# First-layer attention: value products grouped by four heads, and the inverse of the softmax sums split between VectorE and GpSimd

## What is computed

```python
q = (x @ Wq + bq)                      # 32 heads of 16
k, v = ctx @ Wk + bk, ctx @ Wv + bv    # 8 heads of 16
scores = einsum('bkgld,bksd->bkgls', q, k) * scale + mask
attn = softmax(scores)
out = einsum('bkgls,bksd->bkgld', attn, v)
x = layer_norm(out @ Wo + bo + x) * gamma + beta
```

## Time and profile before

| | |
|---|---|
| median of 3 runs | 2901.85 us (2900.69 to 2907.3) |
| the profiled execution | 2904.45 us, its span 2902.6 us |
| granted PE clock, mean of the span | 0.963 |
| busy over the span | PE 94%, DVE 62%, ACT 52%, POOL 45% |
| first-layer loop, batch 0 | from about 53 to 331 us |
| first-layer loop, batch 1 | from about 1500 to 1775 us |

### The profile page before, as it was taken

How to read it: one execution, slowest core, us unless ns; L and a number is a source line. 1 busy time by engine, 2 the same in 40 slices (tenths; PEclk the granted TensorE clock), 3 DMA queues, 4 the chain that set the end, 5 groups by cost and what they waited for, 6 DMA issues and landing times.

```text
span 2902.6 us, 50288 instructions
## 1 busy us (share of the span) xinstructions
PE 2717.9 (94%) x17432; PEld 2168.3 (75%) x17432; DVE 1785.8 (62%) x2626; ACT 1518.5 (52%) x2360; POOL 1312.9 (45%) x710
## 2 busy tenths in 40 slices
PE   6999979999978999997979999899999789999979
PEld 5666668888866888886856666688888668888867
DVE  5999765665645665664159997566566456656541
ACT  3888534455434455543438884445554344554533
POOL 2720036566533566654428101356665335665633
PEclk8999989999998999998979999899999899999989
DMA  8410004435321344441463000135444124454512
GB/s 202 133 43 2 31 20 123 112 101 127 104 66 45 101 121 108 122 115 50 160 133 130 33 2 30 38 105 125 103 126 112 44 53 115 99 128 104 126 37 79
DMA packets 87732, 261.94 MB, mean 90 GB/s; under 512 B 19697, under 2 KB 33281, under 8 KB 81169
## 3 DMA queue, kind: packets, MB, share of 16 engines
q1 hardware_dynamic: 87568, 259.80, 34.2%
HBM read 135.45 MB, written 6.83 MB: 49 GB/s over the span
## 4 chain that ended last, share of the span: by engine, by line
issue 53%; POOL 32%; PE 9%; DMA 2%; DVE 2%; SPq 1%; POOLq 1%; ACT 0%; DVEq 0%; ACTq 0%
POOL pT L459 15%; POOL wa L459 5%; PE ps_m L902 4%; POOL v L459 4%; PE ps_s L902 3%; POOL wo L459 2%; POOL acc L511 2%; POOL wob L507 2%; DMA scr_q<-parts 1%; PE ps_m L1139 1%; POOL x_res L482 1%; DMA acc<-in_rows 1%; SPq L337 1%; DVE hT L1377 0%; POOL z L534 0%
## 5 line engine op out<-in xcount | busy, mean ns | idle before, releaser
L459 POOL TENSOR_TENSOR pT<-pT,pT 128x1024 fp32r<-128x1024 f32 x224 | 538.9, 2407 | 510.5 <-ACT pT L605 509.5
L732 ACT ACTIVATE p<-ps_s,nm 128x1024 f32<-128x1024 f32 x256 | 283.9, 1109 | 292.6 <-DVE nm L1509 292.4
L605 ACT ACTIVATE pT<-pT 128x1024 fp32r<-128x1024 f32 x224 | 237.8, 1062 | 360.1 <-DMA pT<-pb 360.1
L902 PE MATMUL ps_s<-kT,qT 128*128 128x512 f32 x1536 | 400.3, 399 | 6.5 <-ACT p L732 5.7
L459 POOL TENSOR_TENSOR wa<-stg_qk,wa 128x1024 fp32r<-128x1024 f32 x80 | 190.5, 2399 | 373.9 <-ACT wa L605 373.9
L1525 DVE STREAM_TRANSPOSE pb<-p 128x1024 f32<-128x1024 f32 x224 | 278.3, 1242 | 110.0 <-ACT p L732 100.5
L902 PEld LDWEIGHTS ps_s<-kT,qT 128*128 128x128 f32 x1536 | 281.8, 190 | 75.8 <-ACT p L732 19.6
L1506 DVE TENSOR_REDUCE nmx<-ps_s 128x1 f32<-128x1024 f32 x256 | 309.4, 1209 | 33.3 <-PE ps_s L902 33.3
L1433 DVE CUSTOM_DVE_ANT_0 sm<-ps_s,mask 128x1024 f32<-128x1024 f32 x256 | 309.2, 1209 | 20.3 <-PE ps_s L1009 12.0
L685 ACT ACTIVATE p<-sm,nm 128x1024 f32<-128x1024 f32 x256 | 293.2, 1145 | 45.1 <-DVE nm L1433 42.2
L1022 PE MATMUL ps_t<-ident,p 128*128 128x128 f32 x2048 | 288.2, 284 | 14.2 <-DVE pt L1441 7.9
(11 more groups left out here) (133 smaller groups left out, 4244.0 us busy)
## 6 DMA issues: line engine op xcount, KB each, us to landing
pT<-pb SPq DMA_DIRECT2D x896, 128.0 KB, 2.4
stg_qk<-in_wqk SPq DMA_DIRECT2D x40, 1024.0 KB, 7.6
stg_vo<-in_wo SPq DMA_DIRECT2D x48, 512.0 KB, 3.5
wob<-in_wo SPq DMA_DIRECT2D x32, 512.0 KB, 3.6
stg_vo<-in_wv SPq DMA_DIRECT2D x32, 512.0 KB, 3.6
q_stack<-scr_q SPq DMA_DIRECT2D x48, 128.0 KB, 4.4
st_ctx<-in_ctxT SPq DMA_DIRECT2D x8, 512.0 KB, 5.7
mask<-in_mask SPq DMA_DIRECT2D x2, 2048.0 KB, 12.7
```

What stands on the lines that cost most here:

```text
L459: return nc.gpsimd.tensor_tensor(out, x, f32(hi), ALU.subtract)
L605: return nc.scalar.activation(out, in_, ACT.Copy)
L732: nc.scalar.activation(p[t % 2][:], ps_s[t % 2][:], ACT.Exp, bias=nm[:, i:i + 1], scale=SCALE1, accum_out=sums[:, i:i + 1]).then_inc(exp_d ...
L902: mm = nc.tensor.matmul(out, lhs(x, c), rhs(y, c), start=start and c == 0 and i == 0, stop=stop and c == n_tiles - 1 and i == 2)
```

## The change

Three things change in the first-layer loop.

1. PE no longer makes one call values0 in each step. In every fourth step (t % 4 == 3) it makes all four calls, 64 matmuls, for the group before. The call with i = 3 stands at the same step as before.
2. DVE inverts the eight sums alone, into a new buffer rz0 (128 x 2 x 8). GpSimd writes r0 from it: it adds a broadcast zero to a broadcast rz0.
3. GpSimd's loop goes over units: value_rows(u), then the wait for rz0 of unit u, then the spread. The value rows stood ahead of everything in one run before.

ACT's wait for the buffer z0 is now on the small inverse.

```diff
+        rz0 = sb("rz0", [P, 2, UNIT], F32)
@@ GpSimd
-                for f in range(V_B):
-                    value_rows(f)
+                u0 = b * UNITS0
+                for u in range(UNITS0):
+                    value_rows(u)
+
+                    pool.wait_ge(rz0_done, u0 + u + 1)
+                    if u >= 2:
+                        pool.wait_ge(rb0_filled, u0 + u - 1)
+                    nc.gpsimd.tensor_tensor(r0[u % 2][:], rz0[:, u % 2, :].unsqueeze(2).to_broadcast([P, UNIT, HD]),
+                                            zero[:].unsqueeze(2).to_broadcast([P, UNIT, HD]), ALU.add)\
+                        .then_inc(r0_done, 1)
@@ ACT
-                        act.wait_ge(r0_done, b * UNITS0 + u - 1)
+                        act.wait_ge(rz0_done, b * UNITS0 + u - 1)
@@ PE
-                    if t >= GROUPS:
-                        values0(t // GROUPS * GROUPS - GROUPS, t % GROUPS)
+                    if t >= GROUPS and t % GROUPS == GROUPS - 1:
+                        for i in range(4):
+                            values0(t // GROUPS * GROUPS - GROUPS, i)
@@ DVE
                 def inverse(u):
                     dve.wait_ge(exp0_done, t0 + (u + 1) * UNIT)
                     if u >= 2:
-                        dve.wait_ge(rb0_filled, u0 + u - 1)
-                    nc.vector.reciprocal(r0[u % 2][:], z0[:, u % 2, :].unsqueeze(2).to_broadcast([P, UNIT, HD]))\
-                        .then_inc(r0_done, 1)
+                        dve.wait_ge(r0_done, u0 + u - 1)
+                    nc.vector.reciprocal(rz0[:, u % 2, :], z0[:, u % 2, :]).then_inc(rz0_done, 1)
```

More of the change, by code:

```diff
@@ L224, in build @@
         t0_filled, t0_copied = [sem(f"t0_filled{q}") for q in range(2)], [sem(f"t0_copied{q}") for q in range(2)]
+        rz0_done = sem("rz0_done")
         pv0_done, r0_done, rb0_filled, rb0_done = sem("pv0_done"), sem("r0_done"), sem("rb0_filled"), sem("rb0_done")
```

## The result

The changed kernel takes 2919.51 us (median of 6 runs, 2915.35 to 2923.04), the kernel before in the same comparison 2900.8 us (6 runs). The ratio is 1.0061, with a 95% interval of 1.0048 to 1.0074: 18.7 us slower. The forecast was 2922, from a median of 2901.85. The profiled execution took 2923.04 us, its span 2921.2.

What follows compares the result with a forecast made beforehand. PE was taken to bound the first-layer attention loop, DVE and ACT close behind. +0.64 us a unit made 9.6, with ends 10.0 per batch, 20.0 for two; 2904.45 + 20.0 = 2924.5, less 2.6 gives 2922; range 2904 to 2936.

Steps and rivals of the forecast that it cites:

- The group, 8.34: Four loop steps with one 64-product block take 8.34 us instead of 8.12, with two DVE steps of 1.74 in the path.
- The block's price, 1.89 for 64: 64 value products in a row on PE take 1.89 us, against 2.28 for four blocks of 16.
- The normalising product, 0.20: On DVE once in two groups, hidden before; now ahead of the maximum that sets the chain, adding 0.20 us.
- The inverse, worth 0: Smaller reciprocal on DVE, 0.17 for 0.94 us: the 0.77 saved falls in DVE's idle time and is worth 0.
- The spread, 0.5 between 0.2 and 1.3: GpSimd's 128x128 addition of spread inputs, taken at 0.5 us; needed some 8 us later, so either end costs 0.
- What is queued behind the new wait, 0: Value rows and weight loads delayed by GpSimd's wait; stg_qk asked for near 300 us, still hidden, cost 0.
- Ends of the loop: Steps 4 to 7 cost nothing (bounds -1 and +1); the end of the loop comes 0.4 us later.
- The sum: Whole kernel: 10.0 us more per batch, 20.0 for two, giving a forecast median of 2922 us.
- PE's busy share: In the loop of the changed kernel, near 93% instead of 99.7%.
- The first rival: Loop: engines even out the bursts, only PE's work counts, 7.73 for 8.12 a group; -24 us, 2878; 8%.
- The third rival: Loop: PE's idle gaps lower its clock, one slow step per group, +74 us on top, 2996; 3%.

Runs made afterwards that it cites:

- the blocks alone: The kernel before with only the products regrouped into blocks of 64, inverse and GpSimd as before: 2921.41 us, ratio 1.0072.
- the added reciprocal: A one-input, 24-column DVE reciprocal added behind each copy: changed kernel 2935.66 us; with one products call a step and the split inverse 2901.85 us.
- in pairs: Two products calls in every second step (32 products): on the kernel before 2902.67 us, on the changed kernel 2891.14 us.
- the two added additions above: 128x112 DVE addition behind each copy, two of them shown: one products call a step with split inverse 2924.84 us; in the changed kernel 2974.34 us.

## Why the prediction was right, step by step

- **The group, 8.34.** Measured 8.34, and each start within 0.05 of the working (transposes 1.50, 3.11, 4.94; scores 5.93; block 6.46). Undoing the blocks gives 16.36 a unit; the blocks alone give 16.97. That two DVE steps are on the path when DVE's step is longer is shown by the added reciprocal (8.65 for 8.66). In the changed kernel itself DVE's chain is the last by 0.06 (0.03 in the working), so there it shares the path with ACT's.
- **The block's price, 1.89 for 64.** The rows have 225.00 to 226.88, 1.88. That longer blocks cost less per product is real: in pairs it comes out as 0.35 a unit. It was lost in the blocks because PE waits for copies between them. That the switch of tile form is what costs is not shown separately; the rows show only the price by length of block.
- **The normalising product, 0.20.** Adding the parts of a unit as predicted gives 17.01, measured 16.98. Moving it away brings 0.20.
- **The inverse, worth 0.** Shown in both flows (2900.75 alone; 2921.41 without it in the blocks). The small reciprocal took 0.19, for 0.17 from the nearest row.
- **The spread, 0.5 between 0.2 and 1.3.** It took 0.40. The single wait at the first unit was 0.18 in batch 0, under the bound of 0.3, but 0.87 in batch 1, over it. The bound was worked out from batch 0 alone; in batch 1 the value rows ended at 1543.0 and PE had come to the transpose by 1542.7. It costs under 1 us and changes nothing in the verdict.
- **What is queued behind the new wait, 0.** stg_qk was asked for at 291 instead of "near 300" and read 50 us later.
- **Ends of the loop.** Steps 4 to 7 were taken at 0, bounds -1 and +1, and steps 8 to 11 at +0.22. From the first scores to the first transpose of the inverse the changed kernel takes 38.3 instead of 39.1 in batch 0 and 39.5 instead of 39.9 in batch 1, the wait of 0.87 included. Over all profiles of this study the first transpose comes between 89.7 and 94.8, so this part scatters. For the last stretch, from the last but one to the last transpose of the inverse, the sum has 0.22 and 0.20 for steps 124 to 127 and 0.4 for the end, 0.8 in all; measured are 9.86 (329.12 to 338.98) instead of 9.26 (321.30 to 330.56), +0.6.
- **The sum.** The forecast was +20.0, all of it in the loops. The loops took +17.3, the medians +18.7 and the span +18.6. The difference of 2.7 in the loops is at the starts (1.7), in the whole units (0.5) and at the ends (0.4). That the medians come closer to 20.0 than the loops do is luck: 1.7 of the span is scatter behind them.
- **A miss:** PE's busy share. The text forecast near 93%; the row has 163.59 of 170, 96%. I divided start-to-start work by the period, while the busy time counts modelled ends that reach into the gaps. A busy share is the wrong row for a forecast of this kind; the starts are the right one.
- **The first rival (only PE's work counts)** named its deciding point as a DVE step of 1.63. A longer DVE step moved the group by twice its own length, but the way down isn't the same, and the prediction overlooked that: ACT's chain is right behind. By the prediction's own terms, with a DVE so fast that ACT never waits for a maximum, ACT copies at 0.76, 2.40 and 1.25 + 1.15 + 0.49 + 1.15 = 4.04; then come 0.75 and 0.44 to the second half of the transposes, 0.49, 0.53 and 1.89, so 8.14. This is an estimate from the prediction's rows, and no run has a shorter DVE step. By it a faster DVE would at best have brought a group back to the 8.12 of the even flow, and the gain below 1.63 wasn't there.
- **The third rival (the clock)** didn't come: the clock was 1.00 over 160 to 330, with some 0.6 of waiting in each group (8.34 - 7.73). Its text looks only behind the loop, though. At the start of the loop in batch 0, where PE has single waits of up to 3.6 us, the mean clock was 0.52, 0.62 and 0.72 in the three stretches of 10 us from 50 to 80 before the change, and 0.66, 0.66 and 0.83 in the changed kernel; eight transposes there took up to 1.97 instead of 1.09. So the loop has a stretch at the lower clock in both kernels, and it belongs to the scatter at the start.

**Still open.** That it is the single bank per half that keeps PE from running ahead is argued from the waits. A second bank wasn't tried: ps_s, ps_t and ps_m fill all eight. Nor was an instruction added on ACT, which would show how close its chain is.

## What to carry to other kernels

Work that is grouped to make the busiest engine cheaper is worth its saving only as long as this engine then loses less in waiting for the engines behind it: here a burst of 1.0 us (32 products) saves PE 0.13 in a pair of steps (4.06 to 3.93) and costs it 0.05 of waiting, and a unit gains 0.35; a burst of 1.9 us saves 0.39 in a group (8.12 to 7.73) and costs 0.61 of waiting, and with the normalising product's 0.20 a unit is 0.61 longer. Work out the period of the new order from start-to-start rows of each engine when it is behind, not from busy shares; do it for every engine that is close (here DVE at 1.74 and ACT at 1.64 against PE's 2.03 a step); and give each small instruction the place where its engine idles. What an instruction costs holds for one order only: the large inverse is free in the even flow and beside a block of 64, and costs 0.31 a unit with pairs.

## What the hardware showed that was not expected

A DVE addition with two inputs from SBUF doesn't run beside a GpSimd addition or multiplication: it took 0.26 alone and up to 1.56 us beside one. Of the 256 added ones 64 were delayed in the even flow and 36 in the blocks, each ending some 0.13 behind a GpSimd instruction, and none of the short ones lies wholly inside one. The trace of the kernel before shows it too, ahead of the loop, where DVE subtracts two SBUF tiles (otherwise 0.69 long). Its timeline:

```profile
19.56 4.55 POOL L459 TENSOR_TENSOR w0q<-stg_qk,w0q 128x2048 fp32r<-128x2048 f32 x1 [4.38 <-ACT w0q L605]
...
20.85 3.81 DVE L1394 TENSOR_TENSOR tmp_lo<-tmp,parts 128x512 f32<-128x512 f32 x1 [1.65 <-ACTq L665]
...
26.08 0.69 DVE L1394 TENSOR_TENSOR tmp_lo<-tmp,parts 128x512 f32<-128x512 f32 x1 [0.23 <-DVE parts L1396]
```

It ends at 24.66, 0.55 behind GpSimd's 24.11, which is its own 0.69 less 0.14; the two added additions above end 0.13 behind, their own 0.26 less 0.13. So in these rows the DVE instruction does its work when the GpSimd instruction is over. A DVE reciprocal with one SBUF input (0.29 throughout) and the maximum with one input from PSUM and one from SBUF (1.21 beside the value rows and without them) weren't delayed. The Trainium skill, GPSIMD Engine Reference, section Specifications, names contention with DVE instructions that have two SBUF inputs; the trace agrees, with 0.26 alone and 0.44 to 1.56 beside GpSimd. The changed kernel has no such DVE instruction inside this loop's steady flow, and no delay of a DVE instruction beside the value rows is seen in its rows.
